# Attention, FFN and two layernorms on one core: q, k, v and output projections with fp16 halves in place of fp32r halves

## The chip, the cores and the metric

The kernel runs on one core of a Trainium2 chip. The metric is the device time of one launch in microseconds (us). The engines named here are PE (TensorE, matrix products), DVE (VectorE), ACT (ScalarE), POOL (GpSimd) and SP (SyncE, which here only issues DMAs).

## The reference

```python
x = _layernorm(x + attn(x, Wq, bq, Wk, bk, Wv, bv, Wo, bo))   # x is (4, 1024, 256), 16 heads of 128
x = _layernorm(x + ffn(x, w_gate, w_up, w_down, s_gate, s_up, s_down))   # 256 -> 1024 -> 256, int8 weights
...
q = proj(Wq, bq) * scale
k = proj(Wk, bk)
v = proj(Wv, bv)
q = apply_rotary(pos, q)
k = apply_rotary(pos, k)
sim = jnp.einsum('bhid,bhjd->bhij', q, k)
sim = jnp.where(causal, -jnp.finfo(sim.dtype).max, sim)
attn = jax.nn.softmax(sim, axis=-1)
out = jnp.einsum('bhij,bhjd->bhid', attn, v)
return out @ Wo + bo
```

All inputs are fp32 (the FFN weights int8), and fp32 accuracy is wanted.

## The kernel before

Each large product is made of three products of halves: an operand is its value rounded to a narrower type (the high half) plus what the rounding left (the low half); high x high, high x low and low x high are summed in PSUM. In the attention products of probabilities with v the halves are fp16. In all others (x with the weights, q with k, attention output with Wo) they are held in fp32r words, a 32-bit type that PE multiplies rounded.

The program runs over 64 heads (4 batches of 16), n = 0 to 63, with one run before (n = -1) and one behind; then the FFN follows in 8 groups of 512 tokens. One call of `run(n, ...)` on each engine has eight slots, s = 0 to 7. Slot s handles score row tile s of head n (128 queries against (s+1)*128 keys), and between these rows each engine has the work of other heads, in an order written out by hand:

- PE: `scores(s)` (L1123); in slots 0 to 3 `chunk` (L1141), q and k of head n+1; `attend` (L1074), probabilities of head n-1 times v; `output` (L1100), the output projection of a pair of heads; `values` (L1163), v of a later pair.
- DVE: `masked_scores` (L853: scale, mask and row maximum), `probs_low` of row s-1 (L863), `output_low` in slots 1 and 7 (L881), `value_low` (L873), `rotate_cos` in slots 1 to 4 (L904), two short instructions for the reciprocal of the row sum (L911, L914), and `add_output` (L897) ahead of some rows.
- ACT: `probs_high` of row s-1 (L665), `output_high` (L633), `value_high` (L645), `softmax` (L656, exp), then `chunk_out` in slots 0 to 3 (L673, twice).
- POOL: the rest of the rotary embedding (L427, L421) and the halves of q and k (L443, L445).
- SP: the DMA transposes of the probabilities.

A score row thus passes PE, DVE, ACT, DVE, ACT, DVE. Three PSUM tiles `S` of two banks hold rows, so PE can be up to two rows ahead. `attend` of the next head may start only when `output_low` has emptied the one bank `O`.

Each head's Wq and Wk slices, and each pair's Wv and Wo slices, come from DRAM as fp32 in every batch and are split again: the high half on ACT (L497, slots 5 and 6 for Wq and Wk), the low half on POOL (L458, L431, L412). For v alone there is a scale: DVE takes the largest weight (`weigh`, L714 and L719, odd heads, slot 5), PE sums over partitions (L1060), DVE makes factors of it (L727, L735, L736). "Even" and "odd" head below mean par 0 and par 1; a pair of heads is one even and one odd.

## Time and profile before

| | us |
|---|---|
| median of 3 runs (lowest to highest) | 1857.92 (1856.61 to 1859.83) |
| the profiled execution's own time | 1852.92 |
| its span, first to last instruction | 1851.1 |
| mean granted TensorE clock, 1 is full speed | 0.991 |

An engine's busy share says how much of the span it had an instruction in work; matmul records overlap by their pipelining. The timeline gives instructions in order of time, with the idle time before them and what ended it. "issue" there means that the profile shows no releaser.

### The profile page before, as it was taken

To read this page: it belongs to the slowest core of one execution; us is meant where nothing else is said; L and a number is where in the kernel's file an instruction comes from. 1 tells how busy PE (TensorE), PEld (TensorE's weight loads), DVE (VectorE), ACT (ScalarE), POOL (GpSimd) and SP (SyncE) were. 2 spreads that over 40 slices of the span, in tenths; PEclk is the share of its full clock that TensorE was granted. 3 is DMA by queue.
4 is the path that set the end of the run, shared out by engine and by line. 5 is a ranking of instruction groups with operands and counts; after the bars stand their busy time and mean duration, and the time that the engine had idled before them with its cause. 6 is when DMAs were issued, how large, how long until landed. Compare 5 with 4: busy or idle time off the path is not lost. (4 is left out here: it accounts for less than half of the span.)

```text
span 1851.1 us, 33747 instructions
## 1 busy us (share of the span) xinstructions
PE 1755.6 (95%) x10464; PEld 1409.7 (76%) x10464; DVE 1564.9 (85%) x3748; ACT 1463.9 (79%) x2658; POOL 1394.8 (75%) x1293
## 2 busy tenths in 40 slices
PE   6899999999999999999999999999999999899997
PEld 4677877777777777777777777777777777668886
DVE  6788888888888888988888888888888889867886
ACT  5788888888888888888888888888888888754443
POOL 4688877778777878888778878787888877624554
PEclk9899999999999999999999999999999999989999
DMA  3756565666665666576666655675666765540001
GB/s 93 165 116 113 111 139 117 122 131 129 118 119 120 142 120 115 114 157 119 120 122 117 138 111 116 141 141 121 119 114 116 156 141 109 104 99 12 24 24 35
DMA packets 638257, 210.01 MB, mean 113 GB/s; under 512 B 609408, under 2 KB 622208, under 8 KB 636672
## 3 DMA queue, kind: packets, MB, share of 16 engines
q1 hardware_dynamic: 614400, 165.91, 47.9%
q10 hardware_dynamic: 23680, 41.95, 7.9%
q8 instruction: 86, 1.41, 0.3%
q14 instruction: 91, 0.75, 0.1%
HBM read 48.40 MB, written 8.39 MB: 31 GB/s over the span
## 5 line engine op out<-in xcount | busy, mean ns | idle before, releaser
L863 DVE SCALAR_TENSOR_TENSOR planes<-S,recip,planes 128x128 f16<-128x128 f32 (+7 forms) x512 | 417.5, 815 | 113.0 <-ACT planes L665 111.3
L656 ACT ACTIVATE S<-p_row,neg_max 128x128 f32<-128x128 f32 (+7 forms) x512 | 381.5, 745 | 138.9 <-DVE neg_max L853 138.8
L665 ACT ACTIVATE planes<-S,recip 128x128 f16<-128x128 f32 (+7 forms) x512 | 378.9, 740 | 101.4 <-DVE recip L914 73.7
L427 POOL TENSOR_TENSOR swap<-swap,sin_t 128x512 f32<-128x512 f32 x256 | 331.5, 1295 | 166.0 <-ACT swap L673 164.9
L853 DVE CUSTOM_DVE_ANT_0 p_row<-S,mask_row 128x128 f32<-128x128 f32 (+7 forms) x512 | 387.0, 756 | 27.0 <-PE S L1123 26.4
L421 POOL TENSOR_TENSOR rot<-rot,swap 128x512 f32<-128x512 f32 x252 | 325.5, 1292 | 53.6 <-DVE rot L904 50.7
L673 ACT ACTIVATE swap<-S,bqk 64x512 f32<-64x512 f32 x512 | 350.8, 685 | 18.6 <-PE S L1141 5.8
L1123 PE MATMUL S<-QKA 128*128 128x512 f32 (+4 forms) x1152 | 261.9, 354 | 10.3 <-DVE planes L863 5.7
L1123 PE MATMUL S<-QKB 128*128 128x512 f32 (+4 forms) x1152 | 260.4, 353 | 0.4 <-DVE planes L863 0.3
L1074 PE MATMUL O<-PT,VA 128*128 128x512 f16 (+3 forms) x1152 | 215.4, 328 | 29.0 <-issue 25.5
L1074 PE MATMUL O<-PT,VB 128*128 128x512 f16 (+3 forms) x1152 | 214.9, 327 | 29.4 <-issue 27.0
L1123 PEld LDWEIGHTS S<-QKA 128*128 128x128 f32 x1152 | 189.6, 191 | 33.6 <-issue 11.5
L1141 PE MATMUL S<-xT,WA 128*128 128x512 f32 x768 | 201.3, 398 | 10.8 <-DVE xT L708 8.4
L1123 PEld LDWEIGHTS S<-QKB 128*128 128x128 f32 x1152 | 189.4, 191 | 21.4 <-issue 1.9
L1163 PEld LDWEIGHTS X<-WV,xT 128*128 128x128 f32 x1500 | 196.2, 191 | 12.4 <-DVE VB L873 0.2
L1163 PE MATMUL X<-WV,xT 128*128 128x256 f32 x1500 | 205.0, 286 | 0.0
L1141 PE MATMUL S<-xT,WB 128*128 128x512 f32 x768 | 199.1, 394 | 0.0
L1074 PEld LDWEIGHTS O<-PT,VA 128*128 128x128 f16 x1152 | 97.6, 98 | 126.7 <-issue 59.3
L1074 PEld LDWEIGHTS O<-PT,VB 128*128 128x128 f16 x1152 | 97.6, 98 | 126.0 <-issue 58.9
L904 DVE SCALAR_TENSOR_TENSOR rot<-S,bqk,cos_t 128x512 f32<-128x512 f32 x256 | 190.1, 742 | 2.4 <-ACT swap L673 2.4
L445 POOL TENSOR_TENSOR QKB<-rot,QKB 128x512 fp32r<-128x512 f32 x128 | 164.5, 1285 | 10.2
L1141 PEld LDWEIGHTS S<-xT,WA 128*128 128x128 f32 x768 | 140.9, 191 | 37.3 <-issue 8.3
(134 smaller groups left out, 2955.5 us busy)
## 6 DMA issues: line engine op xcount, KB each, us to landing
w_raw<-in_w_heads ACTq DMA_DIRECT2D x64, 256.0 KB, 2.9
wv_raw<-in_w_heads ACTq DMA_DIRECT2D x32, 256.0 KB, 3.4
PT<-planes SPq DMA_TRANSPOSE x512, 3.4
wo_raw<-in_wo_heads ACTq DMA_DIRECT2D x32, 256.0 KB, 2.6
attn_d<-resid ACTq DMA_DIRECT2D x4, 1024.0 KB, 6.3
x_raw<-in_x_cols SPq DMA_DIRECT2D x3, 1024.0 KB, 5.9
resid<-in_x_rows ACTq DMA_DIRECT2D x3, 1024.0 KB, 5.3
resid<-in_x_rows SPq DMA_DIRECT2D x2, 1024.0 KB, 6.8
```

The lines of the kernel that those rows point to most:

```text
L421: nc.gpsimd.tensor_tensor(rot[:, c, :], rot[:, c, :], swap[:, c, :], ALU.add).then_inc(rot_done, 1)
L427: nc.gpsimd.tensor_tensor(swap[:, c, :], swap[:, c, :], sin_t[:, half], ALU.mult).then_inc(sin_done, 1)
L656: nc.scalar.activation(row_psum(n, s)[:, 0:cols], p_row[:, k % 2, 0:cols], ACT.Exp, bias=neg_max[:, s:s + 1], scale=-1.0, accum_out=row_su ...
L665: nc.scalar.activation(row_halves(n, s)[:, 0], row_psum(n, s)[:, 0:cols].rearrange("p (j q) -> p j q", q=P), ACT.Copy, scale=recip[:, s:s ...
L673: nc.scalar.activation(swap[lo:lo + D // 2, c, :], row_psum(n, c)[hi:hi + D // 2, GQ:], ACT.Identity, bias=bqk[hi:hi + D // 2, c % 2, m % ...
L853: nc.vector.tensor_tensor_reduce(row_view(p_row[:, k % 2, 0:cols], s), score_view(row_psum(n, s), s), row_view(mask_row[:, N - cols:], s), ...
L863: nc.vector.scalar_tensor_tensor(halves_of[:, 1], row_psum(n, s)[:, 0:cols].rearrange("p (j q) -> p j q", q=P), recip[:, s:s + 1], halves_ ...
L904: nc.vector.scalar_tensor_tensor(rot[:, c, :], row_psum(n, c)[:, GQ:], bqk[:, c % 2, m % H:m % H + 1], cos_t[:, half], ALU.add, ALU.mult). ...
L1074: last = mm(O[:, first * P:], buf[:, pv, j, who], PT[g][:, j, pp, first:, :].rearrange("p i q -> p (i q)"), start=j == 0 and z == 0, stop= ...
L1123: last = mm(row_psum(n, s)[:, z * GQ:z * GQ + b - a], QK[par][:, 0, part_q, s * P:(s + 1) * P], QK[par][:, 1, part_k, a:b], start=(part_q, ...
L1141: last = mm(row_psum(n, c)[:, GQ:], W[nxt][:, c % 2, pw, t, :], xT[:, px, t, half], start=i == 0 and t == 0, stop=i == 2 and t == KT - 1)
L1163: last = mm(v_psum(n, i)[:, t2, :], xT[:, px, t, tok], WV[:, pw, t, :, :].rearrange("p h c -> p (h c)"), start=z == 0 and t == 0, stop=z = ...
```

## The change

- x, Wq and Wk, Wv, Wo, q, k and the attention output become two fp16 halves, `xT`, `W`, `WV`, `WO`, `QK` and `OT`. To keep them in fp16's range they are scaled by bounds taken on the chip: of x once for each batch (`take_x`, `scale_x`), of Wq and Wk for each head (`weigh_w`, `sum_w` on PE, `take_w`, `scale_w`), of Wv and Wo for each pair (`weigh_v`, `take_v`, `scale_v`, `weigh_wo`, `take_wo`, `scale_wo`).
- Weights are scaled in place on POOL (`w_scale` and two like it), and split as before, but only in batch 0. The halves are written to DRAM (`w_d`, `wv_d`, `wo_d`) by SP and loaded ready made in batches 1 to 3. There the factors of all heads are made at once (`scale_x`, `weigh_all`, `scale_out`).
- The high halves of Wq and Wk move from slots 5 and 6 of ACT to slots 1 and 2 (batch 0 only).
- The row maximum's factor becomes a value for each partition (`to_score`), where it was a number in the instruction; `add_output` now multiplies too; the factor of `output_high` and `output_low` becomes a number.
- Some 1 MB loads and stores are cut into quarters that stand in different slots. The FFN's arithmetic is the same; its tiles lie in the same bytes under other names.

```diff
-MASKED = -1e38
+MASKED = -1e33
...
+DOWN = 2.0 ** -16
...
+    w_d = nc.dram_tensor("w_d", (H, P, 4 * KT * P), F16).ap()
+    wv_d = nc.dram_tensor("wv_d", (H // 2, P, 4 * KT * P), F16).ap()
+    wo_d = nc.dram_tensor("wo_d", (H // 2, P, 4 * DIM), F16).ap()
...
+    xT = at(AT_X, "xT", [P, 2, KT, N])
+    W = [at(AT_W + 4096 * i, f"W{t}", [P, 2, 2, KT, P]) for i, t in enumerate("AB")]
+    WV = [at(AT_WV + 2048 * i, f"WV{t}", [P, 2, KT, 2, P]) for i, t in enumerate("AB")]
+    QK = [at(AT_QK + 16384 * i, f"QK{t}", [P, 2, 2, N]) for i, t in enumerate("AB")]
+    OT = [at(AT_OT + 8192 * i, f"OT{t}", [P, 2, N]) for i, t in enumerate("AB")]
...
+            def keep_w(m):
+                sp.wait_ge(w_lo, n_w(m, 1))
+                sp.dma_start(w_d[m], W[m % 2][:, :, :, :, :].rearrange("p q a t c -> p (q a t c)")).then_inc(w_kept[m % 2], 16)
...
-                    if s == 0 and n >= 1 and n + 2 < HEADS:
-                        w_low(n + 2, par, 0)
-                        w_low(n + 2, par, 1)
...
+            def w_scale(m):
+                pool.wait_ge(wq_scaled, 5 * m + 2)
+                raw = w_raw[m % 2][:, :, :, :].rearrange("p q t c -> p (q t c)")
+                nc.gpsimd.tensor_scalar(raw, raw, sw[:, m:m + 1], None, ALU.mult).then_inc(w_up, 1)
...
-                        w_high(1, 1, s - 3)
-                    if n == 0 and s in (1, 2):
-                        w_high(2, 0, s - 1)
-                    if n >= 0 and n + 3 < HEADS and s in (5, 6):
-                        w_high(n + 3, nxt, s - 5)
...
+                    if n == 0 and s in (2, 3):
+                        w_high(2, s - 2)
+                    if 1 <= n < H - 2 and s in (1, 2):
+                        w_high(n + 2, s - 1)
+                    if par == 0 and s == 4 and own and n // 2 + 1 < H // 2:
+                        wv_high(n // 2 + 1)
...
+            def load_w_halves(m):
+                act.wait_ge(chunked, n_four(m - 2, 3))
+                for i in range(2):
+                    act.wait_ge(w_kept[i], n_two(H - 2 + i))
+                act.dma_start(W[m % 2][:, :, :, :, :].rearrange("p q a t c -> p (q a t c)"), w_d[m % H]
+                              ).then_inc(w_loaded[m % 2], 16)
...
-                nc.scalar.activation(OT[q][:, 0, o], O[:, :], ACT.Copy, scale=pv_down[:, slot:slot + 1]
+                nc.scalar.activation(OT[q][:, 0, o], O[:, :], ACT.Copy, scale=1.0 / UP
...
+            def weigh_w(m):
+                dve.wait_ge(W_in[m % 2], n_two(m))
+                wait(dve, wq_summed, m - 1)
+                nc.vector.tensor_reduce(wq_max[:, m % 2:m % 2 + 1], w_raw[m % 2][:, :, :, :].rearrange("p q t c -> p (q t c)"),
+                                        AX.X, ALU.max, apply_absolute_value=True).then_inc(wq_abs, 1)
+            def take_w(m):
+                dve.wait_ge(wq_summed, m + 1)
+                ts(gw[:, m:m + 1], w_sum(m), 1e-9, 1.0 / UP, ALU.max, ALU.mult).then_inc(wq_scaled, 1)
+            def scale_w(m):
+                one = slice(m, m + 1)
+                dve.wait_ge(wq_scaled, 5 * m + 1)
+                nc.vector.reciprocal(sw[:, one], gw[:, one]).then_inc(wq_scaled, 1)
+                dve.wait_ge(x_scaled, 2)
+                ts(one_x[:, :], gw[:, one], gx[:, 0:1], None, ALU.mult).then_inc(wq_scaled, 1)
+                dve.wait_ge(wq_scaled, 5 * m + 2)
+                ts(bqx[:, 0, :, m], bqk[:, :, m], sx[:, 0:1], sw[:, one], ALU.mult, ALU.mult).then_inc(wq_scaled, 1)
+                dve.wait_ge(wq_scaled, 5 * m + 3)
+                stt(to_score[:, 0, one], one_x[:, :], -SCALE / DOWN ** 2, one_x[:, :], ALU.mult, ALU.mult
+                    ).then_inc(wq_scaled, 1)
...
+            def scale_v(pair):
+                one = slice(pair, pair + 1)
+                dve.wait_ge(scaled, 5 * pair + 2)
+                nc.vector.reciprocal(sv[:, one], gv[:, one]).then_inc(scaled, 1)
+                nc.vector.reciprocal(one_b[:, :], bu[:, 0, one]).then_inc(scaled, 1)
+                dve.wait_ge(scaled, 5 * pair + 4)
+                dve.wait_ge(x_scaled, 1)
+                ts(v_up[:, 0, one], one_b[:, :], gx[:, 0:1], gv[:, one], ALU.mult, ALU.mult).then_inc(scaled, 1)
...
+            def take_x(b):
+                dve.wait_ge(x_summed, b + 1)
+                ts(gx[:, b % 2:b % 2 + 1], x_sum(b), 1.0 / UP, 1.0 / UP, ALU.mult, ALU.add).then_inc(x_scaled, 1)
+                if b:
+                    ts(bu[:, b % 2, :], v_bounds(b), 1e-30, 1.0 / UP, ALU.max, ALU.mult).then_inc(batched, 1)
...
+                    if 0 <= n < H - 3 and s == (1 if n else 2):
+                        weigh_w(n + 3)
+                    if 0 <= n < H - 3 and s == 4:
+                        scale_w(n + 3)
+                    if par == 0 and s == 1 and own and n // 2 + 1 < H // 2:
+                        scale_v(n // 2 + 1)
+                    if par == 1 and s == 5 and (n + 3) // 2 < H // 2:
+                        weigh_v((n + 3) // 2)
+                    if par == 1 and s == 2 and own and n < H:
+                        weigh_wo(n // 2)
+                    if par == 1 and s == 5 and own and n < H:
+                        scale_wo(n // 2)
+                    if n % H == H - 4 and 0 < n < HEADS - H and s == 3:
+                        weigh_all(n // H + 1)
+                    if n % H == H - 3 and 0 < n < HEADS - H and s == 1:
+                        scale_x(n // H + 1)
+                    if n > 0 and n % H == 0 and n < HEADS and s == 0:
+                        scale_out(n // H)
...
-                                               -SCALE, -MASKED, ALU.add, ALU.min,
+                                               to_score[:, n // H % 2, n % H:n % H + 1], -MASKED, ALU.add, ALU.min,
...
-                nc.vector.scalar_tensor_tensor(OT[q][:, 1, o], O[:, :], pv_down[:, slot:slot + 1],
-                                               OT[q][:, 0, o].bitcast(F32), ALU.mult, ALU.subtract
+                nc.vector.scalar_tensor_tensor(OT[q][:, 1, o], O[:, :], 1.0 / UP,
+                                               OT[q][:, 0, o], ALU.mult, ALU.subtract
...
-                nc.vector.tensor_tensor(into, into, X[:, :], ALU.add).then_inc(added, 1)
+                pair = (n - 2) // 2
+                if pair < H // 2:
+                    dve.wait_ge(wo_scaled, 3 * pair + 3)
+                else:
+                    dve.wait_ge(out_scaled, pair // (H // 2))
+                stt(into, X[:, :], of_pair(pv, pair), into, ALU.mult, ALU.add).then_inc(added, 1)
...
+            def sum_w(m):
+                pe.wait_ge(wq_abs, m + 1)
+                if m == 0:
+                    pe.wait_ge(ones_in, 1)
+                    pe.wait_ge(babs_in, 1)
+                mm(w_sum(m), ones[:, :], wq_max[:, m % 2:m % 2 + 1], start=True, stop=False)
+                mm(w_sum(m), ones[:, :], babs[:, m:m + 1], start=False, stop=True).then_inc(wq_summed, 1)
...
-                    if makes_v(n) and par == 0 and s == 1:
-                        bound_of((n >> 1) + 1)
+                    if n == 0 and s == 0:
+                        sum_w(2)
+                    if n < H - 3 and s == 4:
+                        sum_w(n + 3)
+                    if par == 0 and s == 1 and n // 2 + 1 < H // 2:
+                        sum_v(n // 2 + 1)
...
-                    if c < 2:
+                    if m >= H:
+                        if c == 0:
+                            pe.wait_ge(w_loaded[m % 2], n_two(m - H))
```

What this does to the order of instructions, at three places. DVE, an odd head of batch 0, from the end of slot 4 to the end of slot 5 (`bo_b` is the folded bias, as before); first before, then now:

```order
L914 RECIPROCAL recip<-sum_down 128x1
L784 TENSOR_TENSOR bo_b<-bo_b,X 128x256
L853 ISA p_row,neg_max<-S,mask_row 128x768
L853 ISA neg_max 128x1
L863 SCALAR_TENSOR_TENSOR planes<-S,recip,planes 128x5x128
L911 TENSOR_SCALAR sum_down<-row_sum 128x1
L914 RECIPROCAL recip<-sum_down 128x1
```

```order
L1242 RECIPROCAL recip<-sum_down 128x1
L913 RECIPROCAL sw<-gw 128x1
L915 TENSOR_SCALAR one_x<-gw,gx 128x1
L917 TENSOR_SCALAR bqx<-bqk,sx,sw 128x2
L919 SCALAR_TENSOR_TENSOR to_score<-one_x 128x1
L1065 SCALAR_TENSOR_TENSOR bo_b<-X,go,bo_b 128x256
L961 TENSOR_SCALAR go<-S 128x1
L1173 ISA p_row,neg_max<-S,mask_row,to_score 128x768
L1173 ISA neg_max 128x1
L1183 SCALAR_TENSOR_TENSOR planes<-S,recip,planes 128x5x128
L1239 TENSOR_SCALAR sum_down<-row_sum 128x1
L1242 RECIPROCAL recip<-sum_down 128x1
```

Five short instructions on factors stand between two rows where none stood. DVE again, an odd head of batches 1 to 3, from the end of slot 5 into slot 6:

```order
L911 TENSOR_SCALAR sum_down<-row_sum 128x1
L914 RECIPROCAL recip<-sum_down 128x1
L714 TENSOR_REDUCE wmax<-wv_raw 128x2
L719 TENSOR_TENSOR bprod<-wmax,xmax 128x2
L897 TENSOR_TENSOR resid<-resid,X 128x512
L853 ISA p_row,neg_max<-S,mask_row 128x896
```

```order
L1239 TENSOR_SCALAR sum_down<-row_sum 128x1
L1242 RECIPROCAL recip<-sum_down 128x1
L1222 SCALAR_TENSOR_TENSOR resid<-X,pv,resid 128x512
L1173 ISA p_row,neg_max<-S,mask_row,to_score 128x896
L1173 ISA neg_max 128x1
```

The two instructions of `weigh` are gone. ACT, an even head of batch 0, slot 1 and the start of slot 2:

```order
L656 ACTIVATE S1,row_sum<-p_row,neg_max 128x256
L673 ACTIVATE swap<-S1,bqk 64x512 x2
L497 ACTIVATE WO<-wo_raw 128x2x256
L665 ACTIVATE planes<-S1,recip 128x2x128
L645 ACTIVATE VA<-X,v_up 128x512
```

```order
L834 ACTIVATE S1,row_sum<-p_row,neg_max 128x256
L856 ACTIVATE swap<-S1,bqx 64x512 x2
L624 ACTIVATE WA_50<-w_rawA 128x256
L624 ACTIVATE WOB<-wo_rawB_60 128x2x256
L843 ACTIVATE planes<-S1,recip 128x2x128
L823 ACTIVATE VA<-X,v_up 128x512
```

The high half of a weight now stands between `chunk_out` and the next `probs_high`; in batches 1 to 3 both copies are gone from there.

## Rows read from the trace of the kernel before

**Rows 1.** Page, part 1: busy time, share of the span, instructions
```profile
PE 1755.6 (95%) x10464; PEld 1409.7 (76%) x10464; DVE 1564.9 (85%) x3748; ACT 1463.9 (79%) x2658; POOL 1394.8 (75%) x1293
```
**Rows 2.** Windows, one pair: stretch, length, busy by engine, PEclk, DMA share, GB/s
```profile
859.10:908.70 49.60, 48.22 (x295) 38.48 (x294) 43.03 (x106) 42.40 (x79) 40.25 (x39) 1.00 0.60 117
```
**Rows 3.** Timeline of DVE (start, length): first row of heads 0, 16, 32, 35, 36
```profile
29.66 0.28 DVE L853 CUSTOM_DVE_ANT_0 p_row<-S,mask_row 128x128 f32<-128x128 f32 x1
...
437.88 0.29 DVE L853 CUSTOM_DVE_ANT_0 p_row<-S,mask_row 128x128 f32<-128x128 f32 x1
...
836.77 0.29 DVE L853 CUSTOM_DVE_ANT_0 p_row<-S,mask_row 128x128 f32<-128x128 f32 x1
...
911.54 0.28 DVE L853 CUSTOM_DVE_ANT_0 p_row<-S,mask_row 128x128 f32<-128x128 f32 x1
...
936.26 0.29 DVE L853 CUSTOM_DVE_ANT_0 p_row<-S,mask_row 128x128 f32<-128x128 f32 x1
```
**Rows 4.** Timeline: output projection, attend; output_low and the attend behind it
```profile
902.87 0.52 PE L1100 MATMUL X<-WO,OTA 128*128 128x256 f32 x3
903.23 0.52 PE L1100 MATMUL X<-WO,OTB 128*128 128x256 f32 x3
...
904.82 1.16 PE L1074 MATMUL O<-PT,VA 128*128 128x384 f16 x9
905.78 1.64 PE L1123 MATMUL S<-QKA 128*128 128x512 f32 x6
...
935.28 0.74 DVE L881 SCALAR_TENSOR_TENSOR OTA<-O,pv_down,OTA 128x512 fp32r<-128x512 f32 x1
...
936.12 1.79 PE L1074 MATMUL O<-PT,VB 128*128 128x512 f16 x12 [1.36 <-issue]
```
**Rows 5.** Timeline, DVE and ACT, an even head's slot 6
```profile
905.17 1.08 DVE L853 CUSTOM_DVE_ANT_0 p_row<-S,mask_row 128x896 f32<-128x896 f32 x1
...
906.30 1.01 ACT L656 ACTIVATE S<-p_row,neg_max 128x896 f32<-128x896 f32 x1 [0.74 <-DVE neg_max L853]
...
907.47 0.15 DVE L911 TENSOR_SCALAR sum_down<-row_sum 128x1 f32<-128x1 f32 x1 [0.27 <-ACT S L656]
...
907.81 1.23 DVE L853 CUSTOM_DVE_ANT_0 p_row<-S,mask_row 128x1024 f32<-128x1024 f32 x1
```
**Rows 6.** Timeline of DVE, an odd head, slot 5
```profile
926.01 0.96 DVE L853 CUSTOM_DVE_ANT_0 p_row<-S,mask_row 128x768 f32<-128x768 f32 x1 [0.60 <-PE S L1123]
...
928.34 0.67 DVE L714 TENSOR_REDUCE wmax<-wv_raw 128x2 f32<-128x512 f32 x1
929.04 0.87 DVE L719 TENSOR_TENSOR bprod<-wmax,xmax 128x2 f32<-128x2 f32 x1
```
**Rows 7.** Timeline of DVE, an even head, slot 2: probs_low behind the Wo copy
```profile
893.86 0.48 DVE L863 SCALAR_TENSOR_TENSOR planes<-S,recip,planes 128x256 f16<-128x256 f32 x1 [0.59 <-ACT planes L665]
```
**Rows 8.** Groups by line: shapes, count, busy us, mean ns, idle before
```profile
L897 DVE TENSOR_TENSOR resid<-resid,X 128x512 f32<-128x512 f32 x128 | 87.5, 684 | 4.8 <-PE X L1100 4.7
L904 DVE SCALAR_TENSOR_TENSOR rot<-S,bqk,cos_t 128x512 f32<-128x512 f32 x256 | 190.1, 742 | 2.4 <-ACT swap L673 2.4
L633 ACT ACTIVATE OTA<-O,pv_down 128x512 fp32r<-128x512 f32 x64 | 43.6, 682 | 0.0
L497 ACT ACTIVATE OTA<-O 128x512 fp32r<-128x512 f32 x4 | 2.3, 584 | 6.7 <-PE O L1208 6.7
L497 ACT ACTIVATE WA<-w_raw 128x256 fp32r<-128x256 f32 x64 | 25.8, 404 | 0.7 <-DMA w_raw<-in_w_heads 0.6
L443 POOL CAST QKA<-rot 128x512 fp32r<-128x512 f32 x124 | 76.2, 615 | 0.0
L445 POOL TENSOR_TENSOR QKA<-rot,QKA 128x512 fp32r<-128x512 f32 x124 | 159.8, 1289 | 9.9
```
**Rows 9.** Timeline of the start, all engines
```profile
8.37 6.22 PE L1141 MATMUL S<-xT,WA 128*128 128x512 f32 x18 [8.37 <-DVE xT L708]
...
14.20 0.16 DVE L719 TENSOR_TENSOR bprod<-wmax,xmax 128x2 f32<-128x2 f32 x1
```

602 lines of the change are left out of this document (415 added, 187 removed).

## The prediction

> **What bounds the kernel now.** I read the page's busy shares first [rows 1]. PE is at 95%, and the change aims at PE, so the quick answer would be a large gain. The other engines are not idle, though: DVE 85%, ACT 79%. A share over the whole span does not say whether PE waits for the others or they for it, so I went to one pair of heads in the steady part. It lasts 49.60 us, with PE busy 48.22, DVE 43.03, ACT 42.40 and POOL 40.25 [rows 2]. Batch 0 takes 437.88 - 29.66 = 408.2 us, batch 1 takes 836.77 - 437.88 = 398.9 us, 49.9 for each pair [rows 3].
>
> How much of PE's 48.22 is needed? The code gives the columns that are streamed for a pair: scores 27,648, q and k 24,576, attend 27,648, values 12,288, output 12,288, in all 104,448. The fp16 attend streams 2304 columns (three matmuls each of 384, 256 and 128) in 905.78 - 904.82 = 0.96 us [rows 4], which is 2.4 columns a ns and leaves nothing for weight loads. At that rate the pair needs 43.5 us. In fp32r three 256-column matmuls start 0.36 us apart [rows 4], 120 ns each for 107 ns of columns. So up to 48.2 - 43.5 = 4.7 us of each pair is what fp32r costs PE beyond the columns.
>
> Does the next wait end later? A score row passes from DVE to ACT and back: row maximum, exp, reciprocal, and only then DVE's next row. In slot 6 of an even head the maximum starts at 905.17, exp at 906.30, the row sum is read at 907.47 after a wait for exp, and row 7 starts at 907.81 [rows 5]: 2.64 us, none of it a wait for PE, and an add_output stood ahead of it. PE's columns of slot 6 take 2.1 us. At the head's start PE itself stands, 1.36 us in the odd-to-even case [rows 4], until output_low has emptied bank O; the profile prints "issue", but output_low ended at 936.02 and the attend starts at 936.12 [rows 4]. This is a ring of DVE and ACT which PE only feeds.
>
> I therefore laid the DVE and ACT instructions of one pair end to end, in the order of the code, with the lengths of the timeline, each starting when its engine is free and its input is there, PE taken as always ready, and without the v bound and the weight copies. The lengths are, for 128 to 1024 columns: row maximum 0.30 to 1.23 us, exp with its sum 0.49 to 1.25, probs_high 0.37 to 1.11, probs_low 0.35 to 1.28; chunk_out 1.42, other copies 0.68 on ACT and 0.74 on DVE, all overlapping the next by 0.1. From one row maximum to the next this gives 3.36, 2.81, 2.95, 2.48, 3.63, 3.03, 2.63, 3.88 us in the even head (24.8) and 2.19, 2.91, 2.95, 3.15, 2.41, 3.06, 2.63, 3.22 in the odd one (22.5): 47.3 for the pair. The traced odd head lasts 24.7 us (911.54 to 936.26 [rows 3]). Its slots 0 to 2 are as in the walk within 0.05 us each; row 5 starts at 926.01, 14.47 us in, against 13.6, after 0.60 us of waiting for PE there and 0.26 before; and the v bound's 1.5 us make up the rest [rows 6]. So **the ring is at most 2.3 us faster than the kernel now**, whatever PE does.
>
> **The change part by part, batches 1 to 3 (24 pairs).**
> PE: fp16 everywhere, 43.5 us for 47.3: it is ahead in all slots by at least 0.6 us in the same walk, and waits about 2 us at each head for O instead. That gives back only PE's lateness, about 1 us a pair.
> The v bound goes: 928.34 to 929.91, 1.5 us in the ring [rows 6]. The weight copies go from ACT; only the Wo copy lay in the ring, where probs_low waited 0.59 us and the walk has 0.1 to 0.2 without the copy [rows 7], so 0.4 us. Both are left out of the 47.3 already.
> add_output as a scalar_tensor_tensor: 742 for 684 ns, four times, 0.2 us, in the 47.3 too [rows 8].
> The row maximum gets its factor from memory. No row shows this instruction with either form. The nearest: 742 against 684 ns, an instruction with and one without such an operand, both of 512 columns from PSUM [rows 8]: +58 ns. The lower bound is 0. Sixteen rows a pair would be 0.93 us, but in slots 0 to 3 the ring waits for ACT (chunk_out), so eight count: +0.46 us.
> output_high and output_low lose such an operand. For ACT, 682 against 584 ns on the same tile size from PSUM [rows 8]: -0.1 us, on the path twice; for DVE 0.06 us, on the path twice: together -0.3 us.
> POOL loses the low halves of weights, about 5 us a pair, beside other work; loads of halves have the same bytes as before and nothing waits for them.
> Sum: 47.3 + 0.46 - 0.3 = 47.5 us against 49.6 to 49.9 [rows 2, 3], **-2.2 us a pair, -53 us in 24 pairs**. Bounds: 0 or 0.93 for the factor and +-0.4 for the walk, -1.4 to -3.0 us a pair, -34 to -72 in all.
>
> **Batch 0 (8 pairs).** Here work is added to the ring. On ACT the high halves of Wq and Wk now stand in slots 1 and 2, where the ring waits for ACT; they were in slots 5 and 6, where ACT waited. 404 ns less the overlap, 0.31 us each [rows 8], four a pair: +1.2 us. Behind them the new maximum over Wq and Wk on DVE, 0.67 us like the one of v [rows 6], is mostly hidden, since DVE would wait there. scale_w in slot 4 is not: four short instructions; sum_down and reciprocal, of which one waits for the other, take 907.81 - 907.47 = 0.34 us together [rows 5], and two of the four don't wait, so 0.4 us, plus some waiting for POOL; I take 0.7 us with take_w, twice a pair: +1.4. For a pair: the Wo maximum (0.6, half hidden) and its factors, +0.8; v's further factors +0.2. The v bound and the Wo copy stay. From the walk's 47.5: + 1.9 (the v bound and its factors) + 0.4 (Wo copy) + 1.2 + 1.4 + 0.8 + 0.2 = 53.4; laid out slot by slot some of it overlaps, 52.5. Batch 0 has 408.2 / 8 = 51.0 now, with the change of batch in it; I take 50.3 for its other pairs. So +2.2 us for 6.5 pairs with all of it: **+15 us**, from +5 to +40, the upper end if the short instructions stall. The product of two values for each partition takes 0.16 us at the start, with POOL idle [rows 9], and 0.87 us with POOL at work [rows 6]; to_score and pv are of that kind.
> The Trainium skill, page "GPSIMD Engine Reference", section "Key points", says that POOL and DVE contend where DVE has two SBUF inputs or is in a 2-port mode. By that rule to_score, bqx and pv would each pay the 0.7 us between those rows, and the reciprocals nothing: 13 x (1.4 - 0.3) + 8 x 0.7 = 20 us more, 1848 in all. The trace agrees as far as the product goes.
> POOL gets four scalings of 128x512 a pair. No row shows them; the bounds are the cast, 615, and the subtraction, 1289 ns [rows 8]: +2.5 to +5.2 us on 40.25 us, under 52.5 either way.
> **Start:** the first chunk begins at 8.37 us [rows 9]. Now it waits for both halves of x, maximum, sum on PE, factors, then the weight halves ahead of x on ACT: I add two maxima, two copies and the short chain, +5 us (3 to 10). **Three changes of batch:** some ten short instructions on DVE, +1 us each, +3. The FFN has the same instructions: 0.
> **Sum:** -53 + 15 + 5 + 3 = -30. The profiled execution has 1852.92 (span 1851.1), so 1823; its median of runs is 5 us higher, 1857.92, so **1828 us**, own range 1800 to 1852.
>
> **The rivals.**
> *PE was the bound after all* (the walk has slack that I don't see). Then 4.7 us a pair come back, 32 x 4.7 = 150 less 23 for the start, the changes of batch and batch 0: about 1730. For it: 95% busy. Against: the walk, and PE's own waits for O. Chance 4%; between this and my range, 1750 to 1800 (factor free, batch 0 cheap), 8%.
> *Batch 0's short instructions all stall behind POOL* (slower than before). scale_w has four in a chain, with nothing of the ring beside it. If each takes about the 0.87 us of the product [rows 6], a head pays 3.1 us, and the pair's factors of Wo another 1.6: 13 x 2.5 + 8 x 1 = 40 us over my sum, 1868. It decides when batch 0 costs more than 45 / 8 = 5.6 us a pair more than now. Against: the reciprocals of single values never show it. Chance 17%.
> *POOL's work on fp16 is slower*: q and k's eight casts and subtractions, 15.2 us a pair; if they double, POOL has 50 us in batches 1 to 3 and 60 in batch 0, and it becomes the bound: 1857.9 + 24 x 0.5 + 8 x 9 = 1942. No row has POOL on fp16. Chance 4%.
> *The change doesn't do what it says*: fp16 matmuls with these operands keep fp32r's pace. PE at 48.2 plus its wait for O gives 49.3 a pair: -14 + 23, 1867. Against: the attend rows. Chance 4%.
>
> **How the numbers follow.** My forecast has 63%, the two faster ones 4% and 8%, the three slower 17, 4 and 4%. About 0.2% (4 us) is what a measurement of this kernel can tell from no change. Of my own 63% some 60 lie beyond it on the fast side and 3 within it; of the stall's 17, 3 end within it. Faster 60 + 12 = 0.72, same 0.06, slower 14 + 8 = 0.22. Eight in ten: down to 1795, and up to 1868 to take in the stall.
>
> **What would show it.** A pair in batches 1 to 3 should last 47.5 us (first row of one even head to the next), with PE busy near 44 and two waits of about 2 us at L1430, DVE without waits for PE in L1173. The row maximum of 1024 columns should be 1.29 us for 1.23. A pair in the middle of batch 0 should last 52 to 53 us, with DVE waiting for ACT's copies in slots 2 and 3. The first row of head 0 should start at about 35 us, the granted clock stay at full speed. Wrong would be: a pair at 45, or bqx, to_score and pv each near 0.8 us, or DVE and PE waiting for POOL.

## The result, and the profile after

The changed kernel takes 1843.32 us (median of 4 runs, 1840.65 to 1846.63), the kernel before 1857.26 us beside it. The ratio is 0.993, with a 95% interval of 0.991 to 0.995: a gain of 14 us where 30 were forecast. The profiled execution of the changed kernel has 1846.63 us with a span of 1844.8, against 1851.1 before; it is the slowest of its four, and the one of the kernel before lies 4 to 5 us below its median, so the traces differ by 6 us only. The balance below adds up to that: of the 24 us that it falls short of the forecast's 30, 8 are this choice of executions.

The page's busy shares, then the windows of one pair of heads in batch 2 and of one in batch 0 (columns as in [rows 2]), then DVE's timeline with the first score row of heads 0, 16, 32, 34, 35 and 36:

```profile
PE 1668.0 (90%) x10508; PEld 1060.6 (57%) x10508; DVE 1606.1 (87%) x3806; ACT 1398.7 (76%) x2514; POOL 1288.4 (70%) x1187
```
```profile
906.26:953.64 47.38, 44.66 (x289) 27.18 (x288) 42.65 (x101) 39.68 (x73) 33.62 (x32) 1.00 0.61 119
...
252.63:305.93 53.30, 47.54 (x311) 29.56 (x310) 48.97 (x127) 42.16 (x79) 44.47 (x42) 1.00 0.81 168
```
```profile
39.55 0.34 DVE L1173 CUSTOM_DVE_ANT_0 p_row<-S,mask_row,to_score 128x128 f32<-128x128 f32 x1
...
470.12 0.35 DVE L1173 CUSTOM_DVE_ANT_0 p_row<-S,mask_row,to_score 128x128 f32<-128x128 f32 x1
...
858.87 0.35 DVE L1173 CUSTOM_DVE_ANT_0 p_row<-S,mask_row,to_score 128x128 f32<-128x128 f32 x1
...
906.26 0.35 DVE L1173 CUSTOM_DVE_ANT_0 p_row<-S,mask_row,to_score 128x128 f32<-128x128 f32 x1
...
931.04 0.34 DVE L1173 CUSTOM_DVE_ANT_0 p_row<-S,mask_row,to_score 128x128 f32<-128x128 f32 x1
...
953.64 0.35 DVE L1173 CUSTOM_DVE_ANT_0 p_row<-S,mask_row,to_score 128x128 f32<-128x128 f32 x1
```

Set against [rows 2, 3], a steady pair fell from 49.6 to 47.38 us (24.78 + 22.60), and PE is busy for 44.66 of them instead of 48.22. The pair in batch 0 lasts 53.30 us; the same heads took 50.25 before (from the first row of head 8, 233.64, to that of head 10, 283.89). The balance, from first rows of heads (those of head 63 are at 1611.79 and 1607.59):

| stretch | before | after | change | forecast |
|---|---|---|---|---|
| start, to the first row of head 0 | 29.66 | 39.55 | +9.9 | +5 |
| batch 0 | 408.2 | 430.6 | +22.4 | +15 |
| batches 1 to 3, to head 63 | 1173.9 | 1137.5 | -36.4 | -53 + 3 |
| the rest, FFN above all | 239.3 | 237.2 | -2.1 | 0 |

The groups by line (shapes, count, busy us, mean ns, idle before) give the price of single operations; the last rows are timeline rows of PE, its waits for bank O at the start of the even and of the odd head:

```profile
L1173 DVE CUSTOM_DVE_ANT_0 p_row<-S,mask_row,to_score 128x1024 f32<-128x1024 f32 x64 | 82.1, 1283 | 0.4 <-issue 0.3
...
L1222 DVE SCALAR_TENSOR_TENSOR resid<-X,pv,resid 128x512 f32<-128x512 f32 x128 | 96.0, 750 | 4.9 <-PE X L1460 4.2 <-issue 0.2
...
L561 POOL TENSOR_TENSOR QKB<-rot,QKB 128x512 f16<-128x512 f32 x128 | 148.2, 1158 | 10.3
...
L578 POOL TENSOR_SCALAR w_rawA<-w_rawA,sw 128x512 f32<-128x512 f32 x7 | 11.0, 1565 | 0.0
```
```profile
906.04 1.79 PE L1430 MATMUL O<-PT,VA 128*128 128x512 f16 x12 [0.88 <-issue]
...
930.27 1.79 PE L1430 MATMUL O<-PT,VB 128*128 128x512 f16 x12 [1.84 <-issue]
```

Where I say below how long a slot lasts, it is the distance from one row maximum to the next in DVE's timeline, slot 0 being the row of 128 columns.

### The profile page after: what moved, and what is told of

Read it like the earlier page. It is cut to its first block and busy times, and to the rows that moved or that the text cites. A ratio compares the mean times of both kernels' runs of the same rounds, so it can differ in the third digit from the quotient of the medians.

```text
span 1844.8 us, 33867 instructions
## 1 busy us (share of the span) xinstructions
PE 1668.0 (90%) x10508; PEld 1060.6 (57%) x10508; DVE 1606.1 (87%) x3806; ACT 1398.7 (76%) x2514; POOL 1288.4 (70%) x1187
## 5 line engine op out<-in xcount | busy, mean ns | idle before, releaser
L1173 DVE CUSTOM_DVE_ANT_0 p_row<-S,mask_row,to_score 128x128 f32<-128x128 f32 (+7 forms) x512 | 416.9, 814 | 12.1 <-PE S L1491 8.5
L856 ACT ACTIVATE swap<-S,bqx 64x512 f32<-64x512 f32 x512 | 349.6, 683 | 22.3 <-PE S L1512 9.3
L1430 PE MATMUL O<-PT,VB 128*128 128x512 f16 (+3 forms) x1152 | 215.3, 328 | 58.6 <-issue 51.5
L1491 PE MATMUL S<-QKA 128*128 128x512 f16 (+4 forms) x1152 | 231.5, 328 | 6.3 <-DVE planes L1183 3.9
L1491 PE MATMUL S<-QKB 128*128 128x512 f16 (+4 forms) x1152 | 230.9, 328 | 4.3 <-POOL QKB L561 2.2
L1512 PE MATMUL S<-xT,WA 128*128 128x512 f16 x768 | 190.1, 385 | 7.6 <-DVE xT L1035 4.7
L1231 DVE SCALAR_TENSOR_TENSOR rot<-S,bqx,cos_t 128x512 f32<-128x512 f32 x256 | 189.9, 742 | 2.0 <-ACT swap L856 2.0
L1512 PE MATMUL S<-xT,WB 128*128 128x512 f16 x768 | 186.8, 379 | 0.0
L561 POOL TENSOR_TENSOR QKB<-rot,QKB 128x512 f16<-128x512 f32 x128 | 148.2, 1158 | 10.3
L561 POOL TENSOR_TENSOR QKA<-rot,QKA 128x512 f16<-128x512 f32 x124 | 143.7, 1159 | 10.0
L1617 PE MATMUL S<-x1T,ffn_w 128*128 128x512 f32 x512 | 127.7, 394 | 3.9 <-DVE x1T L891 3.2
```

What stands on the lines that cost most here:

```text
L561: nc.gpsimd.tensor_tensor(q[:, c % 2, 1, half], rot[:, c, :], q[:, c % 2, 0, half], ALU.subtract).then_inc(rot_lo, 1)
L856: nc.scalar.activation(swap[lo:lo + D // 2, c, :], row_psum(n, c)[hi:hi + D // 2, GQ:], ACT.Identity, bias=bqx[hi:hi + D // 2, m // H % 2, ...
L1173: nc.vector.tensor_tensor_reduce(row_view(p_row[:, k % 2, 0:cols], s), score_view(row_psum(n, s), s), row_view(mask_row[:, N - cols:], s), ...
L1430: last = mm(O[:, first * P:], buf[:, pv, j, who], PT[g][:, j, pp, first:, :].rearrange("p i q -> p (i q)"), start=j == 0 and z == 0, stop= ...
L1491: last = mm(row_psum(n, s)[:, z * GQ:z * GQ + b - a], QK[par][:, 0, part_q, s * P:(s + 1) * P], QK[par][:, 1, part_k, a:b], start=(part_q, ...
L1512: last = mm(row_psum(n, c)[:, GQ:], W[nxt][:, c % 2, pw, t, :], xT[:, px, t, half], start=i == 0 and t == 0, stop=i == 2 and t == KT - 1)
```

## Experiments: what bounds a steady pair

All ratios are to the kernel before, run on the same chip; the changed kernel's own is 0.993 (0.991 to 0.995).

**PE relieved, in the kernel before and in the changed one.** The same edit in both:

```
-                    for part_q, part_k in ((0, 0), (0, 1), (1, 0)):
+                    for part_q, part_k in ((0, 0), (0, 1)):
...
-                                      stop=part_q == 1)
+                                      stop=part_k == 1)
```

In the kernel before:

> The kernel before with the same pass left out: in fp32r 36 matmuls of 256 columns at 120 ns, 4.3 us of PE less in a pair. The ring theory: only PE's lateness comes back, about 1 us a pair (49.6 to 48.6), 30 us in all, and a pair can't fall under 48.4. Rival, PE was the bound before: 4.3 us a pair, 138 us shorter.

Measured: 1825.42 us, ratio 0.985 (0.983 to 0.987), 28 us less. A steady pair lasts 25.14 + 23.18 = 48.3 us. PE is busy for 3.6 us less in each pair (44.62 for 48.23) and the pair lost 1.3.

In the changed kernel:

> The changed kernel with the third pass of the scores left out (q low x k high): 9,216 columns of 104,448 less for PE in a pair, 3.8 us. The ring theory: PE had slack everywhere, so a steady pair stays at 47.38 us and the run within 3 us. Rival, PE still bounds after the change: 3.8 us x 32 pairs = about 120 us shorter.

Measured: 1838.34 us, ratio 0.992 (0.990 to 0.994), a steady pair 24.78 + 22.47 = 47.25 us, 0.13 less, with PE busy for 3.2 us less. After the change this much of PE's work is free. Both runs fit the ring of DVE and ACT; the rival with PE as the bound wanted 138 and 120 us.

**The bound of v taken out of batches 1 to 3 of the kernel before.**

```
+                if pair >= H // 2:
+                    nc.vector.tensor_reduce(wmax[:, 0:1], wv_raw[:, 0, 0, 0:8], AX.X, ...).then_inc(w_abs, 1)
+                    return
```

> The kernel before, where from pair 8 on the maximum of Wv is taken over 8 values and the product with the maxima of x is left out (the bound of batch 0 serves). The ring theory: slot 5 of the odd head, 4.15 us, becomes about 3.0, 24 times: 26 to 36 us shorter. Rival, PE fills the slot (it is late there by 0.6 us, and its work stays): under 0.6 us a pair, less than 14 us in all.

Measured: 1833.52 us, ratio 0.989 (0.987 to 0.991), 20 us less, between what the theory (26 to 36) and the rival (under 14) wanted. Slot 5 of the odd head went from 4.15 to 3.32 us, not to 3.0: the rows behind it now wait for PE, as DVE's timeline of that kernel shows:

```profile
968.29 0.96 DVE L857 CUSTOM_DVE_ANT_0 p_row<-S,mask_row 128x768 f32<-128x768 f32 x1 [0.60 <-PE S L1127]
...
971.61 1.09 DVE L857 CUSTOM_DVE_ANT_0 p_row<-S,mask_row 128x896 f32<-128x896 f32 x1 [0.26 <-PE S L1127]
```

**The weight copies taken out of batches 1 to 3 of the kernel before** (`copy(W[buf][:, q, 0, 0, 0:8], w_raw[:, q, 0, 0:8])` in place of the whole, for Wv and Wo likewise).

> The kernel before, where from batch 1 on ACT's copies for the high halves of Wq, Wk, Wv and Wo move 8 values a partition in place of 256 or 512 (the halves are then stale). As the prediction has it: only the Wo copy, in slot 1 of the even head, lies in the ring, 0.4 us a pair, 10 us in all; slots 4 to 6, where the others stand, keep their lengths. Rival, every copy counts: 4 x 0.31 + 0.6 + 0.4 = 2.2 us a pair, 53 us.

Measured: 1852.02 us, ratio 0.999 (0.998 to 1.000). Slot 2 of the even head did lose its 0.43 us (3.38 to 2.95), and slot 3 took them back (2.74 to 3.17): the pair stayed at 49.5 us. The copies of q, k and v cost nothing, and the one of Wo only where PE is not late. So the gain of the change is not quite a sum of separate gains. The bound of v alone gave 0.8 us a pair, PE alone 1.3, the copies none, 2.1 together. The change gives 2.2 although its factor from memory costs 0.30 (next experiment), so 0.4 us a pair, by this estimate, comes only with PE out of the way; the shorter output_high and output_low are in it.

**The row maximum with a constant factor.**

```
-                                               to_score[:, n // H % 2, n % H:n % H + 1], -MASKED, ALU.add, ALU.min,
+                                               -SCALE, -MASKED, ALU.add, ALU.min,
```

> The changed kernel with one edit: the row maximum takes its factor as a constant (-SCALE) instead of from memory; all factors are still computed (the scores so get a wrong scale). My theory, the ring of DVE and ACT: the instruction gets 58 ns shorter (1.28 to 1.23 us at 1024 columns) and eight of a pair's sixteen count, so a steady pair goes from 47.38 to 46.9 us and the whole run is 15 us shorter, about 1828. Rival, every row counts: 30 us shorter. Rival, DVE's row maximum is not on the path (PE or ACT alone sets the pace): no change.

Measured: 1829.48 us, ratio 0.987 (0.984 to 0.991). The instruction itself lost the 59 ns, shown by the group by line of that kernel against the first one above:

```profile
L1173 DVE CUSTOM_DVE_ANT_0 p_row<-S,mask_row 128x1024 f32<-128x1024 f32 x64 | 78.4, 1224 | 0.4 <-PE S L1491 0.3
```

A steady pair went to 24.60 + 22.48 = 47.08 us: 0.30 less where 0.46 was expected, so five rows of sixteen count and not eight: those of slots 5 to 7 of the even head and 6 and 7 of the odd one got 0.05 to 0.07 us shorter each, the others none. By the ratios that is some 10 us of the kernel.

## Experiments: batch 0

**Small maxima.** The maxima over Wq, Wk and Wo read 8 values of 512 (`w_raw[m % 2][:, 0, 0, 0:8] if m > 2`, `wo_raw[pair % 2][:, 0, 0:8]`).

> The changed kernel, where the maxima over Wq and Wk (from head 3 on) and over Wo are taken over 8 values a partition instead of 512: 0.15 for 0.69 us each, 13 and 8 of them. As the prediction has it (the first mostly hidden, that of Wo half): slot 2 of the odd head of batch 0 0.3 us shorter, 2 to 4 us in all. Rival, all of them lie in the ring: 13 x 0.54 + 8 x 0.54 = 11 us. Batches 1 to 3 stay at 47.38 us a pair under both.

Measured: 1843.1 us, ratio 0.994 (0.993 to 0.996), batch 0 at 430.6 us as before the edit. Slot 1 of both heads lost 0.5 us and slot 2 gained them back. They are hidden, even more than I had said.

**Small maxima and small copies.** From head 3 on ACT's high halves of Wq and Wk also take 8 values (`if m > 2: into, raw = into[:, 0:8], raw[:, 0:8]`).

> The changed kernel with the small maxima (8 values a partition) and, from head 3 on, ACT's copies for the high halves of Wq and Wk on 8 values too. The maxima alone moved 0.53 us from slot 1 to slot 2 and gained nothing. Theory: DVE's maxima and ACT's copies stand side by side in slots 1 and 2, each hides the other, and only both together free the slots: slots 1 and 2 of the even heads of batch 0 from 6.41 to about 5.7 us, of the odd ones from 8.48 to about 7.7, 9 us in all. Rival, a third thing holds them (POOL's hold on DVE's short instructions, the copies of bv): under 3 us.

Measured: 1841.72 us, ratio 0.994 (0.993 to 0.996). Slots 1 and 2 of the even head have 6.20 for 6.41 us together, those of the odd head 8.27 for 8.48: 0.21 us each, which is what a copy loses (0.42 to 0.21; it costs 0.21 even for 8 values). The size of the copies is a small part of it. That the rest of ACT's own chain (probs_high, output_high, exp, chunk_out) holds the slots of the even head is argued and not shown; slot 2 of the odd head is held by something else, as the next run shows. With the copies out of both slots, in the run with the late copies below, slots 1 and 2 still take 6.11 and 8.43 us.

**The copies of bv go to ACT.**

```
-                    if folds(n) and s == 2:
-                        wait(dve, folded, (n - 3) >> 1)
-                        for tile, h in ((ident, n - 3), (bv_wide, n - 2)):
-                            nc.vector.tensor_copy(...).then_inc(bv_ready, 1)
...
+                    if n > 0 and folds(n + 1) and s in (5, 6):
+                        if s == 5:
+                            wait(act, folded, (n - 2) >> 1)
+                        tile, h = ((ident, n - 2), (bv_wide, n - 1))[s - 5]
+                        copy(tile[:, :], bv_t[:, h:h + 1].to_broadcast([P, P])).then_inc(bv_ready, 1)
```

> The changed kernel with the two copies that spread the bias of v over ident and bv_wide taken from DVE (slot 2 of the odd heads of batch 0, 0.72 + 1.30 us) to ACT (slots 5 and 6 of the even head before). The prediction's sum for batch 0 left them out. If that is what its 53.3 us a pair has over the forecast 52.5, slot 2 of the odd heads falls from 5.21 to 3.5 to 4.0 us and batch 0 gets 8 to 12 us shorter. Rival, slot 2 waits for ACT's copies of weights and chunks, not for DVE: under 2 us.

Measured: 1835.65 us, ratio 0.990 (0.988 to 0.992); batch 0 lasts 423.6 us, 7.0 less, and slot 2 of the odd head 3.34 us for 5.21, of which slot 5 takes back 0.6: 1.2 us a pair. These copies stood in the kernel before as well, but my walk of a pair, made in batch 2, did not hold them, and I built batch 0 on that walk. The timelines of DVE and then POOL in slot 2 of head 9 of the changed kernel (the row at 289.50 is the one that is held up):

```profile
287.03 0.69 DVE L955 TENSOR_REDUCE wo_max<-wo_rawA 128x1 f32<-128x512 f32 x1
287.63 0.72 DVE L1142 COPY ident<-bv_t 128x128 f32<-128x128 f32 x1
288.27 1.31 DVE L1142 COPY bv_wide<-bv_t 128x128 f32<-128x128 f32 x1
289.50 0.74 DVE L1173 CUSTOM_DVE_ANT_0 p_row<-S,mask_row,to_score 128x512 f32<-128x512 f32 x1
```
```profile
287.00 1.27 POOL L517 TENSOR_TENSOR rot<-rot,swap 128x512 f32<-128x512 f32 x1 [0.85 <-DVE rot L1231]
288.22 1.28 POOL L523 TENSOR_TENSOR swap<-swap,sin_t 128x512 f32<-128x512 f32 x1
```

Two equal copies take 0.72 and 1.31 us: POOL's first instruction ends at 288.27, its second at 289.50, and the copies end with them (288.35 and 289.58).

**Factors behind row 0.** one_x, bqx, to_score and the product for v are moved from slots 4 and 5 to slot 0 of the even head.

```
+                    if par == 0 and s == 0 and 2 <= n < H - 2:
+                        if n // 2 + 1 < H // 2:
+                            product_v(n // 2 + 1)
+                        factors(n + 1)
+                        factors(n + 2)
```

> The changed kernel, where in batch 0 the three factors of Wq and Wk that no engine needs at once (one_x, bqx, to_score) and the product of the maxima for v stand behind the row maximum of slot 0 of the even head, where POOL is idle and DVE waits 0.8 us for probs_high, instead of in slots 4 and 5 beside POOL. Theory, such an instruction waits for the end of POOL's: bqx 0.46 and the product 0.87 us fall to 0.2 to 0.3, slot 4 of the even head from 4.00 to 3.7, of the odd from 3.65 to 3.1, slot 5 of the odd from 3.95 to 3.2: 1.5 us a pair, 8 to 10 us in all. Rival, slot 0 of the even head grows by what the others lose (six instructions of 0.2): under 3 us.

Measured: slot 4 of the even head lasts 3.54 us for 4.00, of the odd head 2.98 for 3.65; slot 0 of the even head stayed at 3.43, so the seven instructions there are hidden. bqx takes 280 ns on average for 461. Slot 5 did not move: the product had cost only 0.16 us there in the changed kernel (next section but one). That is 1.15 us a pair; batch 0 lasted 426.9 us, 3.7 less, since head 9 had a long stretch of the kind told at the end of the account of the prediction. In the whole run (1841.39 us, ratio 0.994, 0.993 to 0.996) it can't be told from the changed kernel.

**The weight copies in slots 6 and 7.**

```
-                    if 1 <= n < H - 2 and s in (1, 2):
-                        w_high(n + 2, s - 1)
+                    if 0 <= n < H - 3 and s in (6, 7):
+                        w_high(n + 3, s - 6)
```

> The changed kernel with ACT's copies for the high halves of Wq and Wk (from head 3 on) in slots 6 and 7 of the head before instead of slots 1 and 2. The prediction charged them 1.2 us a pair there. Theory: in slots 6 and 7 ACT waits anyway, slots 1 and 2 of batch 0 get 0.3 us shorter each: 7 to 9 us in all. Rival: DVE's own chain of factors fills those slots, and the copies then add to slots 6 and 7, where exp and probs_high stand in a row: no gain, or 2 us lost. (Shrinking the maxima alone moved 0.53 us from slot 1 to slot 2, so something else holds slot 2: the copies, by the theory.)

Measured: 1868.42 us, ratio 1.008 (1.006 to 1.010), by the ratios 28 us more than the changed kernel; batch 0 alone lasts 456.5 us for 430.6. Slot 7 of the even head grew from 3.82 to 7.6 us. Neither theory had looked at POOL, whose scaling the copy waits for; in the even head POOL is 4 us behind its slot. POOL's row and then ACT's:

```profile
287.66 1.56 POOL L578 TENSOR_SCALAR w_rawB<-w_rawB,sw 128x512 f32<-128x512 f32 x1
```
```profile
289.26 0.42 ACT L624 ACTIVATE WB<-w_rawB 128x256 f16<-128x256 f32 x1 [4.03 <-POOL w_rawB L578]
```

## Experiments: start and change of batch

**The start mended.** The tables come scaled, and the first halves of Wv are made one slot earlier.

```
-            for table in (cos_t, sin_t):
-                nc.gpsimd.tensor_scalar(table[:, :], table[:, :], DOWN, None, ALU.mult).then_inc(tables, 1)
...
-                    if n < 0 and s == 2:
+                    if n < 0 and s == 1:
                         wv_high(0)
```

> The changed kernel with its start mended: the RoPE tables come already scaled (no POOL scalings of 2.8 and 3.2 us beside DVE's x low halves), and the halves of the first Wv are made one slot earlier on ACT and DVE. Theory: x low takes 1.22 for 1.70 us, twice, and PE's 2.9 us of waiting for Wv's low half at 27.2 us go: the first row starts at 35.5 to 37 us for 39.55. Rival, the time is PE's half pace (matmuls of 512 columns every 0.45 us until 24 us): no more than 1 us.

Measured: the first row starts at 34.13 us, 5.4 earlier, but the whole run takes 1844.31 us (ratio 0.995, 0.994 to 0.997). In its trace batch 3 lasts 365.2 us for 361.8 and head 9 29.2 for 27.0, with the same code there (head 58 takes 28.0 us at a mean granted clock of 0.94). PE's timelines of the start, of the changed kernel, then of the one with the light scores (whose start is the same code), then of this one and of the kernel called best3 below, with the same mended start:

```profile
15.12 2.72 PE L1512 MATMUL S<-xT,WA 128*128 128x512 f16 x6 [4.74 <-DVE xT L1035]
...
20.77 6.43 PE L1512 MATMUL S<-xT,WA 128*128 128x512 f16 x18
30.06 2.79 PE L1539 MATMUL S<-WVA,xT 128*128 128x256 f16 x24 [2.86 <-DVE WVA L1077]
```
```profile
15.43 2.72 PE L1512 MATMUL S<-xT,WA 128*128 128x512 f16 x6 [4.46 <-DVE xT L1035]
...
19.85 4.04 PE L1512 MATMUL S<-xT,WA 128*128 128x512 f16 x18
```
```profile
14.47 2.72 PE L1509 MATMUL S<-xT,WA 128*128 128x512 f16 x6 [3.90 <-DVE xT L1032]
...
18.51 4.04 PE L1509 MATMUL S<-xT,WA 128*128 128x512 f16 x18
22.39 2.78 PE L1536 MATMUL S<-WVA,xT 128*128 128x256 f16 x24
```
```profile
19.48 5.43 PE L1510 MATMUL S<-xT,WA 128*128 128x512 f16 x18
```

The first chunk starts 6.75 us later than in [rows 9], and runs at 0.45 us a matmul of 512 columns, half of full pace, while the granted clock of the window reads 1.00 (third number from the end):

```profile
15.00:25.00 10.00, 9.50 (x29) 4.79 (x30) 6.29 (x19) 2.73 (x4) 5.18 (x5) 1.00 0.01 2
```

The next three chunks take 6.43 us in one execution and 4.04 in another of the same code; with the wait at 30.06, 2.86 us, that makes the rest of the 9.9. The kernel before has a slow pace there too: its 18 matmuls in [rows 9] take 0.35 us each, for 0.26 in its later chunks. First rows of eight further kernels with the unmended start lie between 36.39 and 39.75 us.

So not all of the 5.4 us is the edit's. Where the three chunks take 4.04 us, the first row starts at 36.39 us with the unmended start and at 34.13 and 33.89 with the mended one; where they take 5.35 to 6.83, at 38.38 to 39.75 and at 36.37 to 36.92. The edit is worth 2 to 3 us, and PE's pace in the one execution the rest. That is less than the intervals of the ratios can tell.

**Sum and factors one slot earlier at the change of batch** (`s == 0` for `s == 1` in `sum_x`, `take_x`, `scale_x` of head 13, 29 and 45, and the sums in the bank of slot 0).

> The changed kernel, where at each change of batch the sum over x and the factors made from it stand in slot 0 of heads 13, 29 and 45 instead of slot 1. In the changed kernel two of these short instructions (128x16 and 128x8 values) took 1.11 and 1.30 us and both ended within 0.03 us of the end of an instruction of POOL. Theory, they wait for POOL's instruction to end: in slot 0, where POOL stands idle, they take 0.2 to 0.3 us, and the head gets 1.5 to 2 us shorter, 4 to 6 us in all. Rival, they are slow by their form (a factor from memory with SBUF inputs): they take over 1 us there too, and the time stays.

Measured: 1837.99 us, ratio 0.992 (0.990 to 0.994), which can't be told from the changed kernel's. In the traces heads 29 and 45 last 23.53 us for 24.47, 0.9 less each. DVE's and POOL's timelines, of the changed kernel and then of this one:

```profile
1176.29 1.11 DVE L998 TENSOR_SCALAR by_x<-gw,gx 128x16 f32<-128x16 f32 x1
1177.32 1.30 DVE L1000 SCALAR_TENSOR_TENSOR v_up<-inv_b,gx,gv 128x8 f32<-128x8 f32 x1
1178.54 0.24 DVE L1002 SCALAR_TENSOR_TENSOR bqx<-bqk,sx,sw 128x32 f32<-128x32 f32 x1
```
```profile
1176.10 1.27 POOL L517 TENSOR_TENSOR rot<-rot,swap 128x512 f32<-128x512 f32 x1 [1.06 <-DVE rot L1231]
1177.32 1.28 POOL L523 TENSOR_TENSOR swap<-swap,sin_t 128x512 f32<-128x512 f32 x1
```
```profile
1170.20 0.18 DVE L998 TENSOR_SCALAR by_x<-gw,gx 128x16 f32<-128x16 f32 x1
1170.31 0.23 DVE L1000 SCALAR_TENSOR_TENSOR v_up<-inv_b,gx,gv 128x8 f32<-128x8 f32 x1
...
1170.62 1.24 DVE L1005 SCALAR_TENSOR_TENSOR to_score<-by_x 128x16 f32<-128x16 f32 x1
```
```profile
1170.52 1.31 POOL L523 TENSOR_TENSOR swap<-swap,sin_t 128x512 f32<-128x512 f32 x1 [5.03 <-ACT swap L856]
```

The same instructions take 0.18 and 0.23 us while POOL is idle, and 1.11 and 1.30 us beside it. And the last of the chain, which had been short, now meets POOL's first instruction, which ends at 1171.83, and ends at 1171.86. It is the hold and not the form; of the expected 1.5 to 2 us a head 0.9 came, and one instruction still ran into it.

**All together.** First four edits, the start, bv on ACT, the late weight copies and the change of batch:

> Four edits of the changed kernel together: the mended start, the copies of bv on ACT, the weight copies in slots 6 and 7, the factors at the change of batch one slot earlier. If they add up: start 5, bv 7, weights 7, change of batch 5, 24 us less than the changed kernel, about 1820. Rival, ACT, which now takes both sets of copies, becomes the later engine in slots 5 to 7 of batch 0: no more than 15 us less.

Measured: 1856.82 us, ratio 1.002 (1.001 to 1.003), with slot 7 of the even heads of batch 0 at 7.8 us: the late copies again. With the loads of x's rows moved as well:

> The kernel of the last text, with the loads of x's rows at the change of batch issued in slots 3 and 5 of heads 15 and 16 (31 and 32, 47 and 48) instead of slots 1, 3, 5, 7 of head 15 (31, 47), where a transposing DMA came 0.9 to 1.1 us late for ACT in the changed kernel (slot 3: 4.38 to 4.62 us for 3.11). Theory, the loads held up the transposes: slot 3 of these heads goes back to 3.1, 1.3 us a change, 4 us in all. Rival, the transposes are late for another reason: slot 3 stays over 4 us.

Measured: 1849.74 us, ratio 0.998 (0.996 to 0.999). Slot 3 of heads 31 and 47 is 3.11 us. In the changed kernel it was 4.62 and 4.38; ACT's row there:

```profile
1230.67 0.58 ACT L843 ACTIVATE planes<-S,recip 128x384 f16<-128x384 f32 x1 [0.89 <-DMA PT<-planes]
```

The two kernels ran on the same chip, and this one is 7 us faster, clear of both intervals. Of the 22 such slots in the traces of the changed kernel and its ten edits without this one, 21 last 3.18 to 5.47 us and one 3.11 (head 31, in the run with the change of batch alone); of the six in the three traces with it, five last 3.11 or 3.12 and one 3.35. So the loads in these slots do make them long. That they do it by holding up the transposes rests on ACT's waits for the DMA alone. Then the edits that held, without the late copies (best3):

> The edits that held, together: the mended start, the copies of bv on ACT, the factors at the change of batch one slot earlier, the loads of x's rows in slots 3 and 5; the weight copies stay in slots 1 and 2. If they add up: start 5, bv 7, change of batch 3, loads 2 to 4, so 17 to 19 us less than the changed kernel, about 1825. Rival: part of it is taken back by stretches at PE's lower clock level and by late transposes, as with the mended start alone (5.4 us earlier at the first row, but no shorter in all): about 1835.

Measured: 1825.99 us, ratio 0.986 (0.984 to 0.987). The time is the sum's, but the kernel before took 1852.43 us beside this run, for 1857.26 beside the changed kernel. By the ratios the gain over the changed kernel is some 13 us, between the sum (17 to 19) and the rival (8). The start alone was counted at 5 for 2 to 3. And with the factors behind row 0:

> best3 with the factors and the product of the second text of this group in slot 0. If the theory of POOL's hold is right, 8 us less than best3, about 1817; if slot 0 grows by what slots 4 and 5 lose, the same as best3.

Measured: 1819.19 us, ratio 0.982 (0.981 to 0.984), batch 0 at 416.4 us. It is 7 us faster than best3 on the same chip, for 8 expected. It beats both kernels, the one before by 33 us and, by the ratios, the changed one by some 20, and does the change's own work in other places.

## Why the prediction was half right

The measured time lies inside the range, but the gain is half of the forecast, and that is clear of noise (the interval gives 9 to 17 us). The steady pair, 53 of the forecast's us, came as worked out. Three other terms were each too small: what the change costs around the steady pairs in batches 1 to 3 (13.6 us short in the traces), batch 0 (7.4) and the start (4.9).

- **What bounds the kernel:** right. A steady pair has 47.38 us where 47.5 was worked out, and slot by slot the walk is within 0.17 us of the trace. PE is 44.7 us busy for 44; its waits for O are 0.88 and 1.84 us, where two of 2 were expected. PE relieved in the changed kernel gave 0.13 us a pair.
- **The factor from memory:** the length was right, +58 ns (1283 for 1225). Of the sixteen rows five count, not eight: +0.30 us for +0.46. The operand that output_high and output_low lose was right too: 589 ns for 682 on ACT, 686 for 748 on DVE.
- **Bound of v and Wo copy:** right as parts of the walk. By themselves, in the kernel before, they are worth 0.8 us and nothing, since PE was late behind them. The 1.5 us of [rows 6] were also a dear case: the product takes 0.87 us there and 0.60 in most pairs of batches 1 to 3.
- **Batches 1 to 3 outside the steady pairs:** the step "three changes of batch, +1 us each" failed. The steady pairs give 51.7 us, and of these 15.2 are lost again. The heads beside the steady ones lasted 7.7 us over the steady length before and last 22.9 us over it now. At the two later changes (heads 27 to 31, 43 to 47) it is 6.1 and 5.8 us for 1.4 and 2.5: heads 29 and 45 with two stalls beside POOL (1.9 us, 0.6 before), the maxima of x at heads 27 and 43 (1.4 each, nothing there before), slot 3 of heads 31 and 47. I had counted instructions at 0.1 us and not asked what POOL does beside them, though [rows 6] showed a product of two values at 0.87 us. That is 8.0 of the 15.2 us. Two stretches to which the sum gave nothing make most of the rest. Heads 16 to 26 have 3.0 us more than before, above all head 17, whose slot 2 takes 5.44 us for 4.26 with the last copies of bv (1.32 and 1.30 us). Heads 59 to 62, near the end, have 5.3 us over the steady length for 2.3. In head 62 the granted clock, a mean of PE's two levels of 1.2 and 2.4 GHz (0.5 and 1), is 0.93, where the prediction had it stay full, and it was 1.00 before; what PE waited for ahead of it no run isolates. The windows of head 62, now and before:

```profile
1581.95:1607.59 25.64, 23.21 (x142) 14.17 (x141) 21.73 (x51) 21.24 (x38) 16.80 (x16) 0.93 0.50 95
```
```profile
1586.63:1611.79 25.16, 23.01 (x142) 18.18 (x141) 21.46 (x52) 21.59 (x39) 18.70 (x17) 1.00 0.51 97
```

- **Batch 0:** the mid pair has 53.3 us for 52.5. The step "from the walk's 47.5" failed: the walk came from batch 2 and had no copies of bv (1.2 us a pair, by the run that moved them). The chain of factors was priced about right (1.15 us a pair by the run that moved it, 1.4 forecast with what stayed), but the maxima cost nothing, and the copies at most 0.4 us a pair where 1.2 were forecast. Of the 22.4 us, 12.6 lie in the four pairs of heads 2 to 9, 3.1 each, and 10.2 in heads 10 to 15 (pairs of 56.5, 54.4 and 53.3 us for 50.25, 52.2 and 51.5); heads 0 and 1 give 0.4 back. The pair of heads 10 and 11 is the dearest, 6.3 us: head 11 now has the maxima of x, two DVE instructions of 1.21 us in slots 1 and 2, beside the whole work on the weights, and I had given that nothing. Its slots 1 and 2 are 2.0 us longer than those of head 9; no run isolates it.
- **The rule of contention:** the prediction worked out 20 us from the page "GPSIMD Engine Reference", section "Key points", of the Trainium skill. The contention is there, but of the three only bqx pays, and less: 0.46 us on average for 0.28 with POOL idle. to_score, which starts when bqx has waited POOL out, takes 0.15, and pv 0.14, in the middle of POOL's TENSOR_SCALAR. Other chains pay more than once: by_x and v_up, one behind the other, paid 1.11 and 1.30. The product for v, 0.87 us in [rows 6], now takes 0.16 in heads 3, 5, 7 and 9, where POOL's TENSOR_SCALAR stands beside it, and 1.04 in head 11 beside a TENSOR_TENSOR. The rival with all of them stalled, 1868, did not come.
- **POOL:** the scaling of 128x512 takes 1.57 to 1.62 us, above my upper bound of 1.29. It hid in 53 us a pair, but it is why the copies couldn't go to slots 6 and 7. The rival "POOL slower on fp16" is refuted: 1158 ns for 1289.
- **Start:** +9.9 for +5. The step "the short chain" failed: two halves of x awaited where one was, PE at half pace for up to four chunks, and Wv's low half 2.9 us late. The edit of tables and Wv shows that its part is 2 to 3 us; what the rest would be without the slow pace is open.

Single heads are 2 to 3 us longer in one execution than in another (head 9: 27.0 us in the changed kernel, 29.1 with the light scores). With the light scores PE's attend came 2.03 us late there behind a transposing DMA, with the DMA share above 1, and the granted clock, full until then, was 0.58, between the two levels, in 4 us behind it. PE's row and the windows, then PE's row in the changed kernel:

```profile
283.47 0.81 PE L1430 MATMUL O<-PT,VA 128*128 128x512 f16 x3 [2.03 <-DMA PT<-planes]
```
```profile
280.00:284.00 4.00, 1.97 (x10) 0.79 (x9) 3.87 (x10) 3.70 (x8) 3.15 (x4) 1.00 1.09 225
284.00:288.00 4.00, 4.00 (x23) 2.97 (x21) 3.68 (x8) 2.32 (x5) 3.92 (x6) 0.58 0.22 44
```

```profile
288.41 0.81 PE L1430 MATMUL O<-PT,VA 128*128 128x512 f16 x3 [1.82 <-DMA PT<-planes]
```

The other traces agree. In six, head 9 lasts 29.0 to 30.4 us: the attend waited 2.01 to 2.72 us for the DMA, and the granted clock was below 1 in the 8 us behind it. In five, it lasts 26.4 to 27.2 us: the attend waited 1.52 to 1.89 us, and the clock stayed at 1.00. Open is why the DMA comes later in one execution than in another.

## What to carry to other kernels

Walk the ring of engines to find the bound, but walk one head of every kind (first batch, last heads of a batch), not only the steady one: here the steady pair was right to 0.1 us and the gain of the whole was off by a factor of two. Short VectorE instructions on more than one value can wait for GpSimd's running instruction; put them together in a slot where GpSimd stands idle, behind an instruction that the next engine needs. Before a copy is moved to a slot where its engine waits, look how late the engine that feeds it is there. And compare kernels by ratios taken side by side: the kernel before had medians from 1852 to 1857 us here.

## What the runs showed of the hardware

- A short DVE instruction on two or more values beside POOL's TENSOR_TENSOR or CAST lasts until that POOL instruction ends: the rows above agree within 0.1 us (0.72 and 1.31 us for two equal copies, 0.18 against 1.11 for by_x, 0.23 against 1.30 for v_up; bqx of two values goes from 0.28 to 0.56). The Trainium skill, page "SBUF — State Buffer", section "Who interferes with whom", has it as an exclusive lock on a shared port pair, held for the whole instruction. The trace agrees beside these two operations. One case it doesn't settle: one_x, of one value, took 0.19 us in the middle of a POOL instruction (268.87, POOL's from 268.17 to 269.33). And beside POOL's TENSOR_SCALAR it differs, though both engines read SBUF, and the measurement stands: neither of these was held to the end. The product of two values took 0.16 there in heads 3, 5, 7 and 9 (299.10, rows below), and DVE's low halves of x at the start took 1.70 us, for 1.28 in the mended start, beside POOL instructions of 2.78 and 3.19.

```profile
299.10 0.16 DVE L931 TENSOR_TENSOR bprod<-wv_max,xmax 128x2 f32<-128x2 f32 x1
```
```profile
298.00 1.56 POOL L578 TENSOR_SCALAR w_rawA<-w_rawA,sw 128x512 f32<-128x512 f32 x1
```

- A factor from memory instead of a constant costs the row maximum 56 to 62 ns at every width from 128 to 1024 columns (288 to 346 ns, 1225 to 1283).
- PE's first chunk ran at 0.45 us a matmul of 512 columns, for 0.22 later, while the granted clock column says 1.00; the three chunks behind it took 4.04 us, full pace, in 3 of 14 traces and 5.35 to 6.83 in the others.
- POOL takes 1.16 us for a subtraction of 128x512 that writes fp16, 1.29 where it writes fp32r, and 1.57 to 1.62 us for a product with a factor from memory.
